# A graph message-passing layer on one core: root on VectorE in batches, a reordered head, projection bias placed in PSUM, source table first

## What is computed

```python
edge_index = stack([src, dst])          # 400000 edges, dst sorted, 12500 nodes x 128
rbf = exp(-(distances[:, None] - centers)**2 / (2*width*width))      # 50 centers
cut = 0.5*(cos(pi*distances/10) + 1) * (distances <= 10)
W = (silu(rbf @ fw1 + fb1) @ fw2 + fb2) * cut[:, None]
messages = (h[src] @ pw + pb) * W
agg = segment_sum(messages, dst)
y = h + (silu(agg @ mw1 + mb1) @ mw2 + mb2)
out = layernorm(x + y)                  # h is x, eps 1e-5
```

## Time and profile before

| | us |
|---|---|
| median of 3 runs | 1214.91 (1213.65 to 1217.35) |
| the profiled execution: its own time | 1215.85 |
| the profiled execution: span on the core | 1214.1 |
| first gather of a tile starts | 79.89 |
| first `messages` starts | 88.88 |
| last `messages` starts | 1186.74 |
| busy: PE / DVE / ACT / POOL | 661.1 / 579.6 / 346.4 / 617.6 |
| mean granted TensorE clock | 0.735 |

### The profile page before, as it was taken

How to read it: one execution, slowest core, us unless ns; L and a number is a source line. 1 busy time by engine, 2 the same in 40 slices (tenths; PEclk the granted TensorE clock), 3 DMA queues, 4 the chain that set the end, 5 groups by cost and what they waited for, 6 DMA issues and landing times.

```text
span 1214.1 us, 12087 instructions
## 1 busy us (share of the span) xinstructions
PE 661.1 (54%) x3533; PEld 569.2 (47%) x3593; DVE 579.6 (48%) x2078; ACT 346.4 (29%) x485; POOL 617.6 (51%) x688
## 2 busy tenths in 40 slices
PE   3943820572855138337454545747556766655673
PEld 3833720461745027226343435636455655544562
DVE  5654920481964038248533533974264343324443
ACT  2941400330422023113222032402233334333332
POOL 2136777126275731733663626674456565655651
PEclk9976765695777558668775767778677877867786
DMA  4944242021114121202142212313132222331110
GB/s 161 317 126 128 55 129 54 16 69 45 46 49 114 52 74 26 76 24 65 49 125 76 61 33 70 88 46 95 56 84 72 70 74 73 90 81 54 46 50 33
DMA packets 56693, 92.63 MB, mean 76 GB/s; under 512 B 12901, under 2 KB 32038, under 8 KB 56618
## 3 DMA queue, kind: packets, MB, share of 16 engines
q1 hardware_dynamic: 37450, 52.08, 14.2%
q0 software_dynamic: 19168, 39.68, 12.9%
HBM read 75.34 MB, written 16.37 MB: 76 GB/s over the span
## 4 chain that ended last, share of the span: by engine, by line
another core or an unknown queue 33%; DVE 24%; PE 18%; issue 11%; ACT 9%; DMA 2%; DVEq 1%; POOL 0%; SPq 0%; ACTq 0%; POOLq 0%
PE ps_sum L728 5%; PE ps_w L719 5%; DVE agg L1090 5%; DVE pairs L908 4%; PE ps_h L710 3%; DVE message L1074 3%; ACT act_t L614 2%; DVE member L1068 2%; ACT L614 2%; ACT L609 2%; ACT square L606 1%; DVE move L906 1%; ACT rbf L609 1%; DVE moves_now L904 1%
## 5 line engine op out<-in xcount | busy, mean ns | idle before, releaser
L513 POOL DMA_INDIRECT gathered<-proj_rows,src_tab x564 | 556.1, 986 | 234.6 <-issue 165.0
L1074 DVE TENSOR_TENSOR message<-ps_w,gathered 128x512 f32<-128x512 f32 x141 | 97.5, 692 | 385.1 <-remote 237.7
L728 PE MATMUL ps_sum<-member,message 128*128 128x64 f32 x1128 | 188.2, 321 | 162.6 <-DVE message L1074 101.4
L728 PEld LDWEIGHTS ps_sum<-member,message 128*128 128x128 f32 x1128 | 178.4, 239 | 172.5 <-DVE message L1074 110.8
L719 PE MATMUL ps_w<-fw_sb,act_t 128*128 128x128 f32 x1128 | 192.9, 325 | 113.3 <-issue 73.3
L614 ACT ACTIVATE act_t<-ps_h 128x512 f32<-128x512 f32 x141 | 82.2, 596 | 573.1 <-remote 443.3
L1090 DVE TENSOR_TENSOR agg<-agg,ps_sum 128x64 f32 x564 | 122.7, 218 | 186.9 <-remote 128.5
L719 PEld LDWEIGHTS ps_w<-fw_sb,act_t 128*128 128x128 f32 x1128 | 194.5, 242 | 36.1 <-issue 21.4
L710 PE MATMUL ps_h<-rbf,fw_halves 128*128 128x256 f32 x564 | 190.0, 463 | 23.9 <-issue 18.6
L1068 DVE TENSOR_SCALAR member<-iota_f,dst_tab,cut_tab 128x64 f32<-128x64 f32 x564 | 177.0, 322 | 1.1 <-issue 0.7
L716 PEld LDWEIGHTS ps_w<-bias_rhs,one_lanes 128*128 128x128 bf16 x141 | 15.2, 108 | 318.1 <-ACT act_t L614 181.5
(11 more groups left out here) (146 smaller groups left out, 539.9 us busy)
## 6 DMA issues: line engine op xcount, KB each, us to landing
dist_bc<-tile_dist SPq DMA_DIRECT2D x70, 256.0 KB
x_ring<-in_x SPq DMA_DIRECT2D x48, 256.0 KB, 4.5
gathered<-proj_rows,src_tab POOLq DMA_INDIRECT x564
proj_rows<-x_ring SPq DMA_DIRECT2D x24, 256.0 KB, 4.6
out_nodes<-x_ring SPq DMA_DIRECT2D x24, 256.0 KB
pair_rows<-pairs SPq DMA_DIRECT2D x4, 640.0 KB
dist_in<-in_edge_weight SPq DMA_DIRECT2D x5, 312.5 KB
src_in<-in_src SPq DMA_DIRECT2D x5, 312.5 KB
```

The source lines that it names most:

```text
L513: nc.gpsimd.indirect_dma_start(out=gathered[:, slot, :], out_offset=None, in_=proj, in_offset=bass.IndirectOffsetOnAxis(ap=table[:, c:c + ...
L728: last = nc.tensor.matmul(ps_sum[m % 2][:, WINDOW * t:WINDOW * (t + 1)], message[:, m % 2, t * P:(t + 1) * P], member[:, m % 2, t, :], sta ...
L1074: V.tensor_tensor(message[:, n % 2, :], ps_w[n % 2][:, :], gathered[:, MACRO * slot:MACRO * (slot + 1), :].rearrange("p t f -> p (t f)"), ...
```

## The change

It has four parts, all in hand-written lists.

1. Root. `scale` leaves POOL's list. DVE does it in `roots`: a first guess from the bits of the variance (a multiply and add on the integer view), then two refinement steps, nine small instructions for a batch of chunks. Batches are `ROOTS`; a batch is done 5 macros after the last of its chunks is due, and `normalise`, the store and the reload of x follow later accordingly.
2. Head. DVE spreads the counts of group 0 ahead of `build_lanes` and the first shift, PE does its matmul after the second projected chunk rather than after the fourth. Bias splitting, the lane scales and the checks of `address_pieces` go behind `clear_empty`; `repeat_biases` goes behind the tables.
3. Projection bias. `pb` is loaded onto all partitions by one DMA; ACT writes it into the PSUM bank (`put_bias`) and PE's projection adds to it. PE first runs four small matmuls on the two banks. The 25 bias matmuls (L683) go. ACT clears `agg` after the projection in five pieces of 2560 columns.
4. Tables. The source table is made, transposed and taken first (`tables_src`, `turn_src`, `take_src`), and POOL's gate at the first macro of a group is `src_taken`: step 21 in place of 23.

```diff
+ROOTS = ((0, 4), (4, 8), (8, 12), (12, 16), (16, 20), (20, 23), (23, 24), (24, 25))
+CLEARED = 5
+def rooted(i):
+    lo, hi = ROOTS[BATCH_OF[i]]
+    return NODE_AFTER[hi - 1] + 5, i - lo
...
@@ SP @@
-            for i, b in enumerate((fb2, mb2, pb)):
+            sp.dma_start(pb_bc[:, 0, :], pb.partition_broadcast(P)).then_inc(pb_loaded, 16)
...
-                    if m == after + 9:
+                    if m == at + 4 + place:
                         store_out(i)
...
@@ POOL @@
-            def scale(i):
-                pool.wait_ge(node_stats, i + 1)
-                step(nc.gpsimd.tensor_tensor(rstd[:, i % RING, :], var_eps[:, i % RING, :], minus_half[:, :], ALU.pow))
-                step(nc.gpsimd.tensor_tensor(shift[:, i % RING, :], minus_mean[:, i % RING, :], rstd[:, i % RING, :],
-                                             ALU.mult))
-                pool.sem_inc(node_scaled, 1)
...
                 prepare(m)
-                nodes(m)
                 k, c = group_of(m)
                 if c == 0:
-                    pool.wait_ge(main.tables_ready, k + 1)
+                    pool.wait_ge(main.src_taken, k + 1)
...
@@ ACT @@
+            def put_bias(i):
+                rows = chunk_nodes(i)[1]
+                nc.scalar.activation(ps_w[i % 2][0:rows, :].rearrange("p (j f) -> p j f", j=CHUNK),
+                                     pb_bc[0:rows, :, :].to_broadcast([rows, CHUNK, P]), ACT.Copy)
...
             for i in range(CHUNKS):
                 if i + 1 < CHUNKS:
                     take_turned(i + 1)
-                nc.scalar.activation(agg[:, WIDE * i:WIDE * (i + 1)], ones_cols[:, 0:WIDE], ACT.Copy, scale=0.0)\
-                  .then_inc(sums_cleared, 1)
...
+                if i + 2 < CHUNKS:
+                    act.wait_ge(proj_copied, i + 1)
+                    put_bias(i + 2)
+            act.wait_ge(const_built, 4)
+            act.wait_ge(biases_split, 1)
+            for part in range(3):
+                nc.scalar.dma_start(bias_lanes[part:part + 1, :, :], bias_parts[0:1, part, :, :])\
+                  .then_inc(bias_placed, 16)
+            for i in range(CLEARED):
...
-                    if m == after + 8:
+                    at, place = rooted(i)
+                    if m == at + 3 + place:
                         normalise(i)
...
@@ PE @@
-                nc.tensor.matmul(ps_w[i % 2][0:rows, :], one_lanes[:, 0:rows], bias_rhs[:, 2, :, :],
-                                 start=True, stop=False, skip_group_check=True)
...
-                if i == 3:
+                if i == 1:
                     pe.wait_ge(const_built, 3)
                     spread_ends(0)
...
@@ DVE @@
+            def roots(first, chunks):
+                of = slice(first % RING, first % RING + chunks)
                 settle()
+                done(V.tensor_scalar(var_eps[:, of, :], mean_var[:, of, :, 1], EPS, None, ALU.add))
+                done(V.tensor_scalar(root_i[:, of, :], var_i[:, of, :], -0.5, ROOT_MAGIC, ALU.mult, ALU.add))
+                for n, (a, b) in enumerate(ROOT_STEPS):
+                    done(V.tensor_tensor(root_sq[:, of, :], root[:, of, :], root[:, of, :], ALU.mult))
...
+            def prepare_first():
+                drop_far(0, 0)
...
+                spread_counts(0)
+                build_lanes()
+                shift_by(0)
+                take_ends(0)
+                find_rows(0)
+                for n in range(1, STEPS):
+                    shift_by(n)
+                    if n == 5:
+                        address_pieces(0)
+                clear_empty(0)
```

More of the change, by code:

```diff
@@ L409, in nodes @@
             def nodes(m):
-                for i, after in enumerate(NODE_AFTER):
-                    if m == after + 9:
+                for i in range(CHUNKS):
+                    at, place = rooted(i)
+                    if m == at + 4 + place:
                         store_out(i)
-                    if m == after + 12 and i + RING < CHUNKS:
+                    if m == at + 7 + place and i + RING < CHUNKS:
                         load_x_again(i + RING)
@@ L560, in _ @@
                                 main.gathered[m % SLOT_MACROS])
-            for m in range(MACROS, NODE_END + 4):
-                nodes(m)
             pool.wait_ge(outside_ready, 1)
@@ L575, in _ @@
                                             general.gathered[j])
-                for i in range(CHUNKS, 2 * CHUNKS):
-                    scale(i)
         @block.scalar
@@ L665, in _ @@
             pe.wait_ge(const_built, 2)
+            for b in ps_w:
+                for half in range(2):
+                    last = nc.tensor.matmul(b[:, 2 * P * half:2 * P * (half + 1)], ident_halves[:, 0:P],
+                                            ident_halves[:, 0:2 * P], start=(half == 0), stop=True,
+                                            skip_group_check=True)
+            last.then_inc(banks_marked, 1)
             def turn(i):
@@ L857, in repeat_biases @@
                 dve.wait_ge(bias_placed, 48)
-                for k in (2, 0, 1):
+                for k in range(N_BIAS):
                     for t in range(CHUNK):
@@ L955, in address_pieces, with flag, check_pieces @@
                                      ALU.max, ALU.min))
+                dve.sem_inc(addressed, 1)
+            def flag(value, limit, op):
+                done(V.tensor_scalar(worse[:, :], value, limit, None, op))
                 done(V.tensor_tensor(bad[:, :], bad[:, :], worse[:, :], ALU.max))
-                dve.sem_inc(addressed, 1)
+            def check_pieces(k):
+                rows = P * min(k + 1, ROW_GROUPS)
+                total = ends[:, rows - 1:rows]
+                done(V.tensor_scalar(held[:, :], left[:, :], float(P), None, ALU.min))
+                flag(splits[:, 3:4], held[:, 0:1], ALU.is_lt)
@@ L1209, in _ @@
                     statistics(i)
+                    roots(i, 1)
 DVE_GENERAL_STEPS = 57
```

176 lines of the change are left out of this document (104 added, 72 removed).

## The result

| | kernel before | changed kernel |
|---|---|---|
| median of 4 runs, us | 1216.13 (1213.65 to 1225.26) | 1269.31 (1263.37 to 1284.46) |
| ratio, 95% interval | 1 | 1.0407 (1.0328 to 1.0485) |
| profiled execution: time, span | 1215.85, 1214.1 | 1267.37, 1265.6 |
| granted TensorE clock | 0.735 | 0.720 |
| busy PE / DVE / ACT / POOL | 661.1 / 579.6 / 346.4 / 617.6 | 637.6 / 587.2 / 358.6 / 577.2 |

The change made the kernel 4% slower; I had forecast 1201 us, and the range ended at 1238.

The account below looks back on a forecast made before the run. POOL's back-to-back gather bursts, hiding PE's results, were taken as the bound. Terms -9 + 2 + 25 - 30 + 1 = -11 us from 1215.85 gave 1205; about -3 more and 0.94 for the profiled run gave 1201 us, range 1168 to 1238.

Parts of the forecast that it names:

- head and first group, to macro 31: Start: first gather at 64 us instead of 79.89, part given back in POOL's first burst; net -9 us (-16 to 0).
- macros 31 to 62: Second stretch: two long bursts now as then, 44 and 36 gathers to be 52 and 28; 0 us.
- macros 62 to 99: Middle: without the roots' pauses bursts grow to 52, 28, 32 and 56 gathers; +25 us (0 to +47).
- macros 99 to 140: End: after the last gate POOL waits slot by slot, short bursts, last 16 macros undisturbed; -30 us (-44 to 0).
- tail: After the last message: two more chunks normalised late, DVE's root slightly longer than POOL's; +1 us (0 to +4).
- root's work on DVE: DVE's 72 added instructions, 14 us, hide in its idle half; uncovered up to 8 us, taken as +2.
- The mechanism: Main loop: others see PE's results late while POOL gathers back to back; first 5 us free, some 15% backlog drains.
- The price of a long burst: Main loop: 48 gathers in a row plus the 45.5 us without gathers, 108.9 us for 12 macros: 9.1 us each.
- The gate-by-gate count: Macros 62 to 98: each burst, 15% drain, then 4.3 us per macro until the gate opens; 333 us against 286.
- the other method: Macros 62 to 98: 10 macros under shifts at 6.7 us, 26 at 9.1; 304 us against 286.
- The signs of being wrong: Messages in long bursts as fast as outside, last stretch keeping 7 us per macro, or first gather after 72 us.
- Rival 4: Root: POOL is held up by the root's two-input instructions on DVE, 9 us more, 1210 us; chance 0.05.

Follow-up runs that it names:

- e1: The changed kernel with the root put back on POOL: 1192.83 us, 0.9895 of the kernel before.
- e2: The kernel before with only the root moved to DVE in batches: 1264.55 us, 1.0513 of the kernel before.
- e4: The changed kernel with POOL held to 4 macros ahead of the messages, not 16: 1012.28 us, 0.8410 of the kernel before.
- e13: The changed kernel, lead 16, plus a 1500-column memset on POOL after every macro's four gathers: 1029.88 us, 0.8416 of the kernel before.
- e7: The changed kernel, lead 16, plus a one-column memset on POOL after every macro's four gathers: 867.65 us, 0.9564 of the kernel before at 906.91.
- e11: The one-column-memset kernel of e7 run again in the third series, kernel before 1199.23 us: 1245.52 us, 1.0371 of it.

## Why the prediction was wrong, point by point

| term | predicted | measured | |
|---|---|---|---|
| head and first group, to macro 31 | -9 (-16 to 0) | -7.5 | 342.26 to 334.77 |
| macros 31 to 62 | 0 | +14.7 | +7.2 less -7.5 |
| macros 62 to 99 | +25 (0 to +47) | +64 | +71.2 less +7.2 |
| macros 99 to 140 | -30 (-44 to 0) | -18.6 | +52.6 less +71.2 |
| tail | +1 | -1.1 | +51.5 less +52.6 |
| root's work on DVE | +2 | none seen | 0.17 us each as sized |

- **Head: right.** The first gather starts at 66.11 (I said 64), the joined pieces come at 57.68 (56), the first message at 82.92 (80), 6 us earlier than before and not 9. One message in place of three gets through in the first burst, as argued, and 7.5 of the 14 us gained on the first gather are left at macro 31.
- **The mechanism: right in the main.** Bursts of 52 and 56 gathers came, with three to four messages in them. What held them apart was the root on POOL (e1, e2), and the holding follows the gathers (e4, e13). "The length of bursts sets the pace" is too simple, as e4's burst of 48 with 11 messages says. Nor are the first 5 us of a burst what is free: ACT fell idle 10.8 us into the burst of the earlier trace rows (1070.40 - 12.06 against 1047.57), and 7.9 us into the one at 622.10.
- **The price of a long burst failed.** This is the step that made the forecast wrong: "48 gathers in a row ... 9.1 us per macro" in the earlier trace rows. That figure was one burst **together with the 45.5 us gap behind it**, in which 8.7 of its 12 macros were done. The new bursts have gaps of 26.0 and 29.7 us, because POOL arrives later at a gate that opens when DVE's tables are ready. The first 9 us of the gap go into the drain (ACT resumed at 699.53), and only four macros fit in the rest: 13.5 us per macro. The gate-by-gate count, which did take the gaps one by one, gave +47, and the other method +18; I took +25 between them, where the better of them was at hand; even it allowed 3.8 macros inside a burst of 68 us, and 3.2 went through.
- **Macros 31 to 62 failed** too, put at 0. "Two long bursts now as then" was true of the count (the first was 48 gathers, not 44), but the gap behind the first, 45.5 us, was now 25.2 us (440.3 to 465.5), with 4 messages in it. That this gap alone made the loss is not shown: e2, with the root moved and nothing else, has such a burst and a gap of 30.1 us and took 263.4 us for these macros, as the kernel before (264.3); e1 took 249.9; both parts together 279.0. Why they do not add up here is open.
- **The end was half right.** The burst after the last gate, the single slots and the quick last 15 macros all came. The slots ran at 6.6 us a macro instead of 5.8; the 5.4 from a window of three macros was too small a sample.
- **The signs of being wrong** named in the prediction did not come: messages inside long bursts stayed slow, the last stretch left 7 us per macro, the first gather came at 66. The term that failed, 8 to 9 us per macro in the middle, had a sign of its own only in the list of what would show it.
- **Rival 4 is out.** The Trainium skill (GPSIMD Engine Reference, section 8, Key points) has GpSimd and VectorE contend for SBUF when VectorE has two inputs. Beside DVE's shifts the trace agrees (1.92 us); beside the root it does not: the six gathers of the changed kernel that overlap a root instruction took 0.94 us, and the mean of all is 971 ns against 986 before.

```profile
L537 POOL DMA_INDIRECT gathered<-proj_rows,src_tab x564 | 547.5, 971 | 329.0 <-issue 169.3 <-DVEq L1032 112.4 <-DVE message L1127 41.4
```

The better question lay in the rows that I quoted: if long bursts cost so much, what does the lead of sixteen macros buy? Nothing waited for gathered data. Followed to its end, the reading would have given the fix as well.

## What to carry to other kernels

A wait that looks like waste on an engine off the path can be what protects the path: before removing it, ask what the engine will do with the time, and what that does to the others. Where an engine issues transfers far ahead of their use, bound its lead (one constant took the changed kernel from 1.04 of the kernel before to 0.84 here, though in the second series a lead of four changed nothing for the kernel before) before tuning anything else. And price a cycle with its gap, never a burst with somebody else's gap.

## What the runs showed of the hardware that I had not expected

- **In one of two conditions, GpSimd's back-to-back indirect DMAs slow PE and hide what it has finished.** ACT stood idle for up to 69.57 us, PE's matmuls came 2.1 us apart, and 1.36 us of other work per four gathers removed nearly all of it. What in the chip carries it (the path of the semaphore updates, PE's instructions, the writing of descriptors) no run separates.
- **It comes and goes.** The kernel before had medians of 1199 to 1222 us in three series, 1216 beside the changed kernel's first runs, and 906 to 907 in two, and within a series its 4 to 13 runs lie within 2.2% of each other. It is not a property of the chip: one chip gave 907 in the second series and 1222 in the fourth. The granted clock goes with it (0.85 and 0.72 for the same program, e7 and e11; PE is busy 71% and 52% of the span). Which follows from which was not tried. What switches it is open. In the one condition the change costs 4%, in the other it gains about 4% if e7 stands for it; a lead of three wins in both.
